# The last attention's softmax: transposed blocks copied by the other engines, row maxima taken in halves

## The reference, cut to what matters

```
def step(h, p):                       # h: (4, 1024, 64)
    op = jnp.argmax(h[0, 0, :NOPS])
    q = h @ p['wq'][op]
    k = h @ p['wk'][op]
    v = h @ p['wv'][op]
    attn = jax.nn.softmax(jnp.einsum('bqd,bkd->bqk', q, k) * scale, axis=-1)
    y = jnp.einsum('bqk,bkd->bqd', attn, v) @ p['wo'][op]
    h = jnp.where(p['am'][op], y, h)
    ...
```

## Time and profile before

| | |
|---|---|
| runs, us | 741.06, 741.99, 745.93; median 741.99 |
| profiled execution: span, us | 740.9 |
| PE busy, share of the span | 605.2 us, 82% |
| DVE busy | 571.3 us, 77% |
| ACT busy | 440.8 us, 59% |
| POOL busy | 470.9 us, 64% |
| mean granted TensorE clock | 0.948 of full speed |

### The profile page before, as it was taken

The page is one execution under the profiler, slowest core; times in us unless marked ns, Lnnn a source line. Parts: engine busy times, 40 slices in busy tenths (PEclk is TensorE's granted clock), DMA queues, the critical chain, the costliest instruction groups (busy, mean ns, idle before and its releaser), DMA issues.

```text
span 740.9 us, 10581 instructions
## 1 busy us (share of the span) xinstructions
PE 605.2 (82%) x3591; PEld 253.3 (34%) x3591; DVE 571.3 (77%) x589; ACT 440.8 (59%) x662; POOL 470.9 (64%) x250
## 2 busy tenths in 40 slices
PE   4876696797896787987777788898889988999997
PEld 2321121121221211221212122245656335777762
DVE  4489999998998998998998999554465545666645
ACT  3887767668587578578577555163545515555532
POOL 6369999999999999999999999650000310000002
PEclk9999789789998998998998999999999999999999
DMA  3389566577576666666675675000000000000001
GB/s 99 85 275 306 227 230 234 199 254 236 201 256 233 210 243 237 223 232 229 207 260 198 242 244 199 21 0 1 3 4 9 1 19 1 2 1 2 2 2 60
DMA packets 33112, 105.35 MB, mean 142 GB/s; under 512 B 6933, under 2 KB 7454, under 8 KB 33054
## 3 DMA queue, kind: packets, MB, share of 16 engines
q1 hardware_dynamic: 31958, 103.94, 41.1%
q10 hardware_dynamic: 776, 0.55, 0.3%
q0 software_dynamic: 320, 0.13, 0.1%
HBM read 98.84 MB, written 2.10 MB: 136 GB/s over the span
## 4 chain that ended last, share of the span: by engine, by line
PE 41%; POOL 16%; DVE 16%; issue 15%; ACT 7%; DMA 3%; DVEq 0%; SPq 0%; POOLq 0%; ACTq 0%
POOL hc L1764 8%; POOL dbu L1775 8%; DVE hh_all L1464 7%; PE py L229 6%; PE pb L198 6%; PE px L252 5%; PE py L727 5%; DVE pb L1459 4%; DMA cc<-scr 2%; PE pb L939 2%; PE px L754 2%; PE pb L715 1%; PE py L963 1%; PE px L242 1%; DVE yg L1473 1%
## 5 line engine op out<-in xcount | busy, mean ns | idle before, releaser
L1764 POOL TENSOR_TENSOR hc<-hh_all,cc 128x1024 f32<-128x1024 f32 x128 | 300.2, 2390 | 2.4 <-DVE hh_all L1464 1.3
L727 PE MATMUL py<-hc,w_cst 64*64 64x512 f32 x1024 | 153.2, 658 | 26.9 <-POOL hc L1764 17.1
L1464 DVE TENSOR_TENSOR_SCAN hh_all<-da,pb 128x1024 f32<-128x1024 f32 x72 | 164.6, 2286 | 2.5
L1778 POOL TENSOR_TENSOR yg<-w_xs 128x512 f32<-128x512 f32 x10 | 12.6, 1266 | 232.6 <-DVE w_xs L1599 142.8
L1464 DVE TENSOR_TENSOR_SCAN hh_all<-pb,dbu 128x1024 f32<-128x1024 f32 x56 | 127.7, 2280 | 17.4 <-POOL dbu L1775 13.9
L1775 POOL TENSOR_TENSOR dbu<-bb,dtu_all 128x1024 f32<-128x1024 f32 x56 | 133.8, 2389 | 0.0
L715 PE MATMUL pb<-bc,w_sel 128*128 128x512 bf16 x144 | 48.2, 420 | 66.1 <-DVE hh_all L1464 63.6
L1184 ACT ACTIVATE pb<-dt_all,w_aneg 128x1024 f32<-128x1024 f32 x56 | 62.6, 1118 | 58.5 <-DVE hh_all L1464 56.9
L1459 DVE TENSOR_TENSOR pb<-pb,dtu_all 128x1024 f32<-128x1024 f32 x72 | 87.5, 1215 | 1.9 <-DVE dtu_all L1445 0.2
L286 DVE TENSOR_REDUCE gate_all<-pb 128x1 f32<-128x1024 f32 (+7 forms) x64 | 60.4, 985 | 29.6 <-PE pb L208 14.9
L1184 ACT ACTIVATE da<-dt_all,w_aneg 128x1024 f32<-128x1024 f32 x72 | 80.5, 1137 | 0.5
(11 more groups left out here) (291 smaller groups left out, 950.3 us busy)
## 6 DMA issues: line engine op xcount, KB each, us to landing
cc<-scr SPq DMA_DIRECT2D x128, 512.0 KB, 4.5
bb<-scr SPq DMA_DIRECT2D x56, 512.0 KB, 4.8
w_xs<-hc SPq DMA_DIRECT2D x6, 256.0 KB, 4.6
w_xst<-in_x SPq DMA_DIRECT2D x2, 512.0 KB, 5.4
scr<-bcf SPq DMA_DIRECT2D x8, 128.0 KB, 3.8
w_xs<-dt_all SPq DMA_DIRECT2D x4, 256.0 KB, 6.1
w_xs<-dtu_all SPq DMA_DIRECT2D x4, 256.0 KB, 5.8
out<-yg SPq DMA_DIRECT2D x4, 256.0 KB, 2.6
```

Source lines behind the costliest of these rows:

```text
L727: last = nc.tensor.matmul(py[part(t), half(r)], ident[part(r), part(r)], hc[u % NHC][part(r), half(t)], start=(n == 0), stop=(n == NS - 1) ...
L1464: nc.vector.tensor_tensor_scan(hh[u % NHH][:, :], decay[:, :], drive[:, :], 0.0, ALU.mult, ALU.add).then_inc(scan_done, 1)
L1764: nc.gpsimd.tensor_tensor(hc[u % NHC][:, :], hh[u % NHH][:, :], cc[u % NCC][:, :], ALU.mult).then_inc(hc_done, 1)
```

## The change

In the attention of the chain only:

- The copies change engines and places. ScalarE copies the first batch's transposes of group g behind both exponentials of g (`act_turned_ahead`), and VectorE copies the second batch's transposes of g-1 behind the maxima of g (`dve_turned_behind`). TensorE's waits before its transposes follow: those of r = 0 wait for VectorE's copies, those of r = 1 for ScalarE's.
- The maxima are taken in halves (`dve_max_halves`): each half of 512 scores has its own signal from the score products (`s_full` counts 4 a group in place of 2), VectorE reduces r = 0 and r = 1 of the first half, then of the second half, and behind each of the latter a 128x1 minimum of the two negated half maxima gives `nm`. `mh` holds the half maxima. Each of the two minima waits for the reduction in front of it, and `nm_done` counts 6 a group.
- `dve_all` and `act_all` lose the branches that only the causal attention's sizes would take.

The order for group g is then: VectorE: output of g-3; four half maxima and two minima of g; both copies of r = 1 of g-1; reciprocals of g. ScalarE: both exponentials of g; both copies of r = 0 of g; spread reciprocals of g-2. TensorE's order stays.

```diff
@@ -84,7 +84,7 @@
             eng.sem_inc(sem, count)
 
     def prime_pe(self, pe):
-        for sem, count in ((self.q_full, 4), (self.k_full, 4), (self.v_full, 4), (self.s_full, 2 * self.GRP),
+        for sem, count in ((self.q_full, 4), (self.k_full, 4), (self.v_full, 4), (self.s_full, 4 * self.GRP),
                            (self.turned, 4 * self.GRP), (self.o_full, self.GRP)):
             pe.sem_inc(sem, count)
 
@@ -93,7 +93,7 @@
             act.sem_inc(sem, count)
 
     def prime_dve(self, dve):
-        for sem, count in ((self.k_out, 4), (self.v_dve, 2), (self.nm_done, 2 * self.GRP), (self.pts_dve, 2 * self.GRP),
+        for sem, count in ((self.k_out, 4), (self.v_dve, 2), (self.nm_done, 6 * self.GRP), (self.pts_dve, 2 * self.GRP),
                            (self.rc_done, self.GRP), (self.o_out, self.GRP)):
             dve.sem_inc(sem, count)
 
@@ -195,10 +195,10 @@
             m = min(HALF, plain - a)
             for r in range(2):
                 rows = slice(C * r, C * r + C)
-                last = nc.tensor.matmul(self.s[r][:, o + a:o + a + m], self.qt[rows, g * 128:(g + 1) * 128],
+                part = nc.tensor.matmul(self.s[r][:, o + a:o + a + m], self.qt[rows, g * 128:(g + 1) * 128],
                                         self.kt[rows, p * L + a:p * L + a + m], start=True, stop=True)
-                if not self.causal and a + m == n:
-                    last.then_inc(self.s_full, 1)
+                if not self.causal:
+                    part.then_inc(self.s_full, 1)
         if self.causal:
             for r in range(2):
                 rows = slice(C * r, C * r + C)
@@ -216,13 +216,17 @@
             pe.wait_ge(self.q_out, 4 * k + 4)
             pe.wait_ge(self.k_out, 4 * k + 4)
         for h, (a, m) in enumerate(self.halves(g)):
-            if r == 0 and not (self.small(g) and self.small(g - 1)):
+            if r == 0 and not self.causal:
+                atleast(pe, self.pts_dve, self.evacs_done(k, g))
+            if r == 1 and not self.causal:
+                pe.wait_ge(self.pts_act, self.evacs_done(k, g) + len(self.halves(g)))
+            if r == 0 and self.causal and not (self.small(g) and self.small(g - 1)):
                 atleast(pe, self.pts_act, self.evacs_done(k, g))
             if r == 0 and self.small(g - 1):
                 atleast(pe, self.pts_dve, self.evacs_done(k, g))
             if r == 1 and self.small(g):
                 atleast(pe, self.pts_act, self.evacs_done(k, g))
-            if r == 1 and not self.small(g):
+            if r == 1 and self.causal and not self.small(g):
                 pe.wait_ge(self.pts_dve, self.evacs_done(k, g) + len(self.halves(g)))
             o = self.turn_start(g, r)
             for j in range(a, a + m, 128):
@@ -286,6 +290,27 @@
         self.nc.vector.tensor_reduce(self.nm[:, i:i + 1], self.s[r][:, self.start(g):self.start(g) + 128 * self.blocks(g)], AX.X, ALU.max,
                                      negate=True).then_inc(self.nm_done, 1)
 
+    def dve_max_halves(self, dve, k, g):
+
+        at = self.GRP * k + g
+        for a in range(2):
+            for r in range(2):
+                dve.wait_ge(self.s_full, 4 * at + 2 * a + r + 1)
+                self.nc.vector.tensor_reduce(self.mh[:, 2 * a + r:2 * a + r + 1], self.s[r][:, HALF * a:HALF * a + HALF], AX.X, ALU.max,
+                                             negate=True).then_inc(self.nm_done, 1)
+                if a == 1:
+                    i = 2 * (g % 2) + r
+                    dve.wait_ge(self.p_done, 2 * (at - 2) + r + 1)
+                    dve.wait_ge(self.nm_done, 6 * at + 3 + 2 * r)
+                    self.nc.vector.tensor_tensor(self.nm[:, i:i + 1], self.mh[:, r:r + 1], self.mh[:, 2 + r:3 + r],
+                                                 ALU.min).then_inc(self.nm_done, 1)
+
+    def dve_turned_behind(self, dve, k, g):
+        for h, (a, m) in enumerate(self.halves(g)):
+            dve.wait_ge(self.turned, self.turns_done(k, g, 1) + h + 1)
+            dve.wait_ge(self.o_full, self.GRP * k + g - 1)
+            self.nc.vector.tensor_copy(self.pts[g % 2][1][:, a:a + m], self.pt[:, a:a + m]).then_inc(self.pts_dve, 1)
+
     def dve_turned(self, dve, k, g):
         for h, (a, m) in enumerate(self.halves(g)):
             dve.wait_ge(self.turned, self.turns_done(k, g, 0) + h + 1)
@@ -304,24 +329,21 @@
                 self.dve_project(dve, k, (0, 1))
             if g >= 3:
                 finish(dve, k, g - 3)
-            if not self.ahead(g):
-                for r in range(2):
-                    self.dve_max(dve, k, g, r)
+            self.dve_max_halves(dve, k, g)
             if g == 0:
                 self.dve_project_v(dve, k, (0,))
                 self.dve_project(dve, k, (2, 3))
                 self.dve_project_v(dve, k, (2,))
-            if self.ahead(g + 1):
-                for r in range(2):
-                    self.dve_max(dve, k, g + 1, r)
-            self.dve_turned(dve, k, g)
+            else:
+                self.dve_turned_behind(dve, k, g - 1)
             self.dve_inverse(dve, k, g)
+        self.dve_turned_behind(dve, k, self.GRP - 1)
         for g in range(self.GRP - 3, self.GRP):
             finish(dve, k, g)
 
 
     def act_exp(self, act, k, g, r):
-        act.wait_ge(self.nm_done, 2 * (self.GRP * k + g) + r + 1)
+        act.wait_ge(self.nm_done, 2 * g + r + 1 if self.causal else 6 * (self.GRP * k + g) + 4 + 2 * r)
         if g >= 2 or not self.causal:
             act.wait_ge(self.turned, self.turns_done(k, g - 2, r) + len(self.halves(g - 2)))
             act.wait_ge(self.rc_done, self.GRP * k + g - 1)
@@ -329,6 +351,12 @@
         self.nc.scalar.activation(self.p[g % 2][r][:, 0:n], self.s[r][:, self.start(g):self.start(g) + n], ACT.Exp, bias=self.nm[:, i:i + 1],
                                   accum_out=self.sm[:, i:i + 1]).then_inc(self.p_done, 1)
 
+    def act_turned_ahead(self, act, k, g):
+        for h, (a, m) in enumerate(self.halves(g)):
+            act.wait_ge(self.turned, self.turns_done(k, g, 0) + h + 1)
+            act.wait_ge(self.o_full, self.GRP * k + g - 1)
+            self.nc.scalar.activation(self.pts[g % 2][0][:, a:a + m], self.pt[:, a:a + m], ACT.Copy).then_inc(self.pts_act, 1)
+
     def act_turned(self, act, k, g):
         o = self.turn_start(g, 1)
         for h, (a, m) in enumerate(self.halves(g)):
@@ -346,23 +374,15 @@
         for g in range(self.GRP):
             if g == 0:
                 self.act_project(act, k, (0, 1))
-            elif not self.small(g - 1):
-                self.act_turned(act, k, g - 1)
-            if not self.ahead(g):
-                for r in range(2):
-                    self.act_exp(act, k, g, r)
+            for r in range(2):
+                self.act_exp(act, k, g, r)
             if g == 0:
                 self.act_project_v(act, k, (1,))
                 self.act_project(act, k, (2, 3))
                 self.act_project_v(act, k, (3,))
+            self.act_turned_ahead(act, k, g)
             if g >= 2:
                 self.act_inverse(act, k, g - 2)
-            if self.ahead(g + 1):
-                for r in range(2):
-                    self.act_exp(act, k, g + 1, r)
-            if self.small(g):
-                self.act_turned(act, k, g)
-        self.act_turned(act, k, self.GRP - 1)
         self.act_inverse(act, k, self.GRP - 2)
         self.act_inverse(act, k, self.GRP - 1)
 
@@ -516,7 +536,7 @@
         bufs = {"qt": u2_all, "kt": dt_all, "vv": xs[:, vv_at:vv_at + T2C].rearrange("p (g r c) -> p g r c", g=T2C // 128, r=2),
                 "p": [[bb[0], bb[1]], [dbu[0], dbu[1]]], "pts": [[da[0], da[1]], [cc[0], cc[1]]],
                 "rs": small[:, 0:256].rearrange("p (a q) -> p a q", a=2),
-                "nm": small[:, 256:260], "sm": small[:, 260:264], "rc": small[:, 264:268],
+                "nm": small[:, 256:260], "mh": small[:, 268:272], "sm": small[:, 260:264], "rc": small[:, 264:268],
                 "s": pb, "pt": py, "ob": px[0], "rb": px[1]}
         at = Attention(nc, ctx, w, True, bufs)
         mask_words = gate_all[0:1, 272:272 + 2 * MASKW].bitcast(I32)
```

More of the change, by code:

```diff
@@ L67, in __init__ @@
                     "pts": [[sb(f"pts_{a}{r}", [128, L]) for r in range(2)] for a in range(2)],
-                    "rs": sb("rs", [128, 2, 128]), "nm": sb("nm", [128, 4]), "sm": sb("sm", [128, 4]), "rc": sb("rc", [128, 4]),
+                    "rs": sb("rs", [128, 2, 128]), "nm": sb("nm", [128, 4]), "mh": sb("mh", [128, 4]), "sm": sb("sm", [128, 4]), "rc": sb("rc", [128, 4]),
                     "s": [ps(f"s_{r}", [128, L]) for r in range(2)], "pt": ps("pt", [128, L]),
@@ L71, in __init__ @@
         self.qt, self.kt, self.vv, self.p, self.pts = (bufs[name] for name in ("qt", "kt", "vv", "p", "pts"))
-        self.rs, self.nm, self.sm, self.rc = (bufs[name] for name in ("rs", "nm", "sm", "rc"))
+        self.rs, self.nm, self.mh, self.sm, self.rc = (bufs[name] for name in ("rs", "nm", "mh", "sm", "rc"))
```

## The result

The changed kernel takes 750.75 us (median of 4 runs, 747.32 to 752.30), the kernel before 741.52 in the runs beside it. The ratio is 1.0106 with a 95% interval of 1.0073 to 1.0138, so it is slower by 0.7 to 1.4%, 5.4 to 10.2 us. (The ratios and intervals in this document are worked out from all runs of both kernels and are not quotients of the medians: 750.75 / 741.52 would be 1.0124.) The profiled execution has a span of 745.5 us.

A forecast was written before the change was run, and what follows sets the result against it. TensorE's nearly gapless order was taken to bound the kernel before, at 6.08 us a group. VectorE's longer chain would add 0.67 + 6.1 + 0.47 - 0.2 = 7.0 us to 742.0, giving 749.0 us, range 744.0 to 753.7.

The forecast's parts named there:

- period of 6.55: Last attention, groups 2 to 14: time per group in the changed kernel, against 6.08 us before (bounds 6.30 and 6.90).
- TensorE bounded the kernel before, ScalarE stood level with it and had nothing to give: Last attention: TensorE nearly gapless at 6.08 us a group; ScalarE's chain ends within 0.2 us; at most 0.1 us to gain.
- The chain from the first half maximum to the transposes, 4.35 us: VectorE's half maxima, minima and copies up to TensorE's first-batch transposes: 4.35 us a group (4.10 to 4.70).
- The four gaps around the minima: VectorE, maximum to minimum twice, minimum to maximum, minimum to copy: 0.45 us together, between 0.20 and 0.80.
- The output loop is level with the first bank of scores: VectorE's output of g-3, waiting for ScalarE, frees the first half maximum 2.20 us behind the transposes; the scores at 2.18.
- "much slower" rival: Output loop through ScalarE or waits around the minima take 0.3 us more: period 6.85 and up, 753.5 us; chance 0.17.
- The ends: Groups outside the regular pattern: group 0 zero, group 1 +0.67 us, group 15 +0.47, and -0.2 behind it.
- the 0.47 a group: Groups 2 to 14: added time per group over 6.08 us (bounds 0.22 to 0.82), 6.1 us for 13 groups.
- The rule on the fixed cost of small instructions: VectorE's halves: each split costs 0.125 us by the rule, some +0.12 a group, 751 us in place of 749.
- The clock: TensorE's new idle time could bring a fall to half clock: 1.8 us at most, included in the range.
- since they write the same two banks: TensorE's first-batch transposes of g wait for both VectorE copies of the second batch's transposes of g-1.
- My sum of 7.0: Whole program: 7.0 us added, from 0.67, 6.1, 0.47 and -0.2, on a median of 742.0 us.

The follow-up runs named there:

- wait_per_bank: Changed kernel; each half of the first batch's transposes waits only for VectorE's copy of its own bank; 744.27 us, ratio 1.0023; second sample 742.49 us, 1.0002; period 6.08.
- halves_only: Kernel before with the maxima taken in halves and nothing else; 742.33 us, ratio 1.0002, period 6.08 us.
- one_copy_back: Changed kernel with the second batch's second-bank copy given back to ScalarE ahead of its exponentials, plus a wait for each bank; run once, 742.63 us, period 6.08.
- before_per_bank: Kernel before, with each half of a set of transposes waiting only for the copy of its own bank; 741.18 us against 741.43, ratio 0.9991.
- output_late: Changed kernel with the output of g-3 moved on VectorE from ahead of the half maxima to behind the reciprocals; run once, period 6.50 us.
- after_again: The changed kernel measured again, unedited, against the kernel before; 750.59 us against 742.58, ratio 1.0108, period 6.50 us.
- copies_only: Changed kernel with whole maxima, so only the exchange of the copies; 753.22 us, ratio 1.0146 against the kernel before, period 6.71 us.
- minima_late: Changed kernel with both minima placed behind all four half maxima; run once, period 6.28 us apart from group 2.
- extra_in_chain: Changed kernel with one more 128x512 VectorE reduction per group from 1 on, between the second minimum and the copies; run once, period 7.00 us.
- extra_behind: Changed kernel with one more 128x512 VectorE reduction per group from 1 on, behind the reciprocals; run once, period 6.50 us apart from one interval.

## Why the prediction was right

I forecast 749.0 us, between 744.0 and 753.7, with a period of 6.55, and the chain on VectorE as the cause. 750.75 and 6.50 were measured. The mechanism held: TensorE waits for VectorE's copies before the first batch's transposes in every group, and not for ScalarE before its scores. By its own steps:

- *TensorE bounded the kernel before, ScalarE stood level with it and had nothing to give.* Right: in `wait_per_bank` ScalarE is done 0.50 before the next scores and the period is still 6.08. `halves_only` frees no time, and a gapless TensorE at 6.08 is what three other orders come back to (`wait_per_bank`, `one_copy_back`, `before_per_bank`).
- *The chain from the first half maximum to the transposes, 4.35 us.* Measured 4.34 (657.13 to 661.47), by two small errors that cancel: the closeness of the sum is luck. The four gaps around the minima, which no row of before showed, are 0.04, 0.10, 0.03 and 0.17: 0.34, not 0.45, nearer to my lower bound of 0.20 than to the upper of 0.80. TensorE's restart behind the last copy took 0.14 to its first product and not 0.05.
- *The output loop is level with the first bank of scores, at 2.20 against 2.18 behind the transposes.* Right: the output starts at 656.92 and holds VectorE for 0.21, until 657.13, which is 2.16 behind the transposes (654.97) and 1.16 behind the scores as well; `output_late` shows that neither is in front. That refutes the "much slower" rival, which I gave 0.17.
- *The ends.* The undisturbed profile (`after_again`) has +0.57 for group 1 (I said 0.67), 5.46 for groups 2 to 14 (6.1), +0.2 for group 15 and behind it (0.27) and -0.1 for group 0 (zero): 6.1 us where I summed 7.0. The term that was too large is the 0.47 a group, measured as 0.42, thirteen times. It is made of 1.02 from the transposes to the scores, measured as 1.00; 1.18 to the first half maximum, measured as 1.16; and 4.35, measured as 4.34.
- *The rule on the fixed cost of small instructions.* Three half maxima lasted 1.88 us, which is 0.60 from start to start and 0.68 for the last. The estimate that I took from the Trainium skill ("VectorE: DVE Perf Modes", section on the TRN2 errata) would have had 0.66, and 751 us; the runs keep to the rows.
- *The clock.* I put one fall of 1.8 us at most into the range and gave it no case of its own. The fall that I read from the earlier trace rows is that of group 0's projections. It was there in 12 of the 13 profiles, of both orders; the last section has the falls that came later.

The part that I did not see at all is how little held the loss. I wrote down that the transposes wait for both copies "since they write the same two banks" and took the wait as given. Asking which of the two banks each half needs would have shown that one of the two waits was needless, and that the change could be had at no cost. It would still have gained nothing: the period is then 6.08, as before.

What stays open: the medians are 8 to 9 us apart (7.9 and 8.0 by the ratios) and the attention of an undisturbed profile 6.1. The interval takes in both, and the two samples of `wait_per_bank` differ by 1.8 us among themselves. My sum of 7.0 lies between the two numbers, and no run says which of them it should be held against. The clock may have a part in it: the six runs of `after_again` have a mean granted clock of 0.938, the 23 of the kernel before beside them 0.943. It isn't the whole account, since the four runs of `copies_only` have 0.947 and their median is also 10.6 us over the kernel before, where the trace shows 9.5 in the attention.

## What to carry to other kernels

When a copy moves to another engine, add up that engine's order from the event that starts it to the event that the consumer waits for; its busy share (69% here) says nothing about it, as the same extra instruction showed, which cost 0.50 us in the chain and nothing behind it. Taking work off an engine that was level with the bound gave nothing here. And look at what a wait covers: waiting for the copy of one bank instead of both took back the whole loss of a reordering that had looked like a bad idea, though it left no gain.

## What the runs showed of the hardware

TensorE's clock fell to half (1.2 GHz) in the first projections of group 0 in 12 of the 13 profiled executions, behind a wait of 2.1 to 2.2 us for weights. From the first projection to the scores of group 0 it is 6.22 to 6.24 us in eleven of them and 6.42 in `before_per_bank`. It is 4.73 in the changed kernel's first profile, which has the same wait (2.13) and no fall there. So a fall cost 1.5 us here, 1.7 in `before_per_bank`, in either order.

Later in the attention the clock fell in 4 of the 13, always behind the long wait of TensorE in group 1: 2.5 us in the changed kernel, 1.8 in `before_per_bank`, 2.3 in `minima_late` and 3.0 in `extra_in_chain`. Waits of 1.8 to 2.8 us in the same place brought none in the other nine. In the changed kernel's first profile, the only one of the four that had no fall in group 0, the windows view reads:

```profile
622.00:623.00 1.00, 1.00 (x5) 0.67 (x5) 0.00 (x0) 0.74 (x2) 0.00 (x0) 0.50 0.00 0
...
624.00:625.00 1.00, 1.00 (x4) 0.34 (x2) 0.38 (x1) 0.00 (x0) 0.00 (x0) 0.61 0.00 0
```

The scores of group 2 take 3.10 us in place of 1.99 there. The fall lengthened groups 1 and 2 by 1.5 us together in this profile, group 2 by 1.4 in `minima_late`, by 1.1 in `extra_in_chain` and by 1.7 in `before_per_bank`, which has the waits of the kernel before. So it is not the change's alone, and whether the longer wait makes it more frequent is not settled by 13 profiles.

In `extra_behind`, `extra_in_chain` and `one_copy_back` one interval of the attention is 0.35, 0.35 and 0.18 us longer than the others. In the first two VectorE pauses for 0.29 us in front of the fourth half maximum, whose scores have been complete for over a microsecond; in the third it pauses for 0.36 us in front of its copy. Nothing in the trace says why.
